# Three-stage layer tower on one core: the attention's output product in column halves with two transposes back to rows, and GpSimd's adds, one expert layer and one transpose moved

## The reference

```python
h = tok(x, mask)                       # running counts per skill, four features, a linear map to 64
h = h + attn(layernorm(h))             # linear attention with decay 0.97
h = h + ffn(layernorm(h))              # 8 experts, the best 2 weighed by a softmax, exact GELU
```

```python
x_t    = l1_normalised(0.97 * x_state + relu(v @ Dx.T))
a_star = rho @ x_t
y_t    = relu(ln(a_star) @ Dy.T) * relu(x_t)
v_star = ln(y_t @ E.T)                 # the product that the change touches
rho    = 0.97 * rho + ln(v)[:, :, None] * x_t[:, None, :]
```

## Time and profile before

| | |
|---|---|
| median of three runs | 813.21 us |
| the profiled execution | 814.54 us |
| its span | 812.7 us |
| TensorE busy | 689.5 us, 85% |
| VectorE busy | 655.8 us, 81% |
| ScalarE busy | 353.4 us, 43% |
| GpSimd busy | 284.0 us, 35% |
| one turn in the middle | 19.21 us |
| granted TensorE clock in that turn | full, the 2.4 GHz level |

### The profile page before, as it was taken

One profiled execution on the slowest core, in us unless ns is written; L12 is line 12 of the kernel. 1 busy time (PEld: TensorE's weight loads), 2 busy tenths in 40 slices (PEclk: granted clock), 3 DMA queues, 4 the chain that ended last, 5 costly groups with the idle time before them and its releaser, 6 DMA issues.

```text
span 812.7 us, 17227 instructions
## 1 busy us (share of the span) xinstructions
PE 689.5 (85%) x4254; PEld 407.6 (50%) x4254; DVE 655.8 (81%) x2531; ACT 353.4 (43%) x787; POOL 284.0 (35%) x333
## 2 busy tenths in 40 slices
PE   2663994067899999999999999999999999999876
PEld 1553663045555555555555555555555555555432
DVE  5998885876888888888888888888888888888752
ACT  4001992012455444445545554444454444445543
POOL 1000000012444444444444444444444444444433
PEclk9999995589999999999999999999999999999988
DMA  7000000101333334433333333333333344342223
GB/s 249 15 0 1 0 0 14 33 27 51 79 81 97 97 93 100 95 110 87 85 85 85 85 85 85 85 85 85 85 93 95 92 100 96 97 104 60 60 61 71
DMA packets 45186, 61.06 MB, mean 75 GB/s; under 512 B 21560, under 2 KB 24108, under 8 KB 44652
## 3 DMA queue, kind: packets, MB, share of 16 engines
q1 hardware_dynamic: 43028, 60.13, 28.8%
q10 hardware_dynamic: 1944, 0.66, 0.4%
q0 software_dynamic: 192, 0.01, 0.0%
HBM read 55.77 MB, written 5.02 MB: 75 GB/s over the span
## 4 chain that ended last, share of the span: by engine, by line
PE 64%; DVE 19%; issue 9%; ACT 2%; DVEq 2%; POOL 2%; DMA 1%; ACTq 0%; SPq 0%; POOLq 0%
PE bank L1257 13%; PE bank L1166 13%; PE bank L1222 6%; PE bank L1178 5%; PE bank L1205 4%; PE bank L1275 4%; PE bank L1250 4%; PE bank L1251 3%; DVE h_all L887 3%; DVE same L663 3%; DVE st_h L893 2%; PE bank L1099 2%; PE bank L1110 2%; PE bank L1155 1%; DVE top L928 1%
## 5 line engine op out<-in xcount | busy, mean ns | idle before, releaser
L512 ACT ACTIVATE skill_rows<-bank,b1T,w_scale 128x512 f32<-128x512 f32 x256 | 194.5, 776 | 52.8 <-PE bank L1251 51.6
L1166 PE MATMUL bank<-feat_parts 128*128 128x256 f32 (+3 forms) x512 | 159.6, 446 | 8.7 <-DVE feat_parts L833 7.6
L407 POOL TENSOR_TENSOR feat_parts<-skill_rows 128x512 f32<-128x512 f32 x64 | 80.9, 1265 | 220.5 <-DVE skill_rows L966 220.5
L485 ACT ACTIVATE feat_parts<-bank 128x384 f32<-128x384 f32 (+2 forms) x96 | 36.7, 383 | 212.0 <-DVE feat_parts L839 209.4
L1257 PE MATMUL bank<-skill_rows,w_sb 128*64 128x512 f32 x256 | 125.4, 611 | 0.2
L1258 PE MATMUL bank<-skill_rows,w_sb 128*64 128x512 f32 x256 | 125.4, 611 | 0.0
L1166 PEld LDWEIGHTS bank<-feat_parts 128*128 128x128 f32 x512 | 90.8, 193 | 50.0 <-issue 20.2
L374 POOL TENSOR_TENSOR same<-h_all,mean_h 128x256 f32 (+1 forms) x32 | 19.5, 608 | 164.7 <-DVEq L1030 164.6
L833 DVE TENSOR_TENSOR_SCAN feat_parts<-same,feat_parts 128x512 f32<-128x512 f32 x64 | 74.6, 1207 | 0.0
L1222 PEld LDWEIGHTS bank<-eT,feat_parts 128*128 128x128 f32 x512 | 64.7, 192 | 4.3
L1222 PE MATMUL bank<-eT,feat_parts 128*128 128x64 f32 x512 | 65.7, 272 | 0.0
(11 more groups left out here) (249 smaller groups left out, 1332.6 us busy)
## 6 DMA issues: line engine op xcount, KB each, us to landing
same<-factor_d SPq DMA_DIRECT2D x32, 512.0 KB, 4.4
skill_rows<-w_d SPq DMA_DIRECT2D x32, 512.0 KB, 6.2
feat_parts<-w_d SPq DMA_DIRECT2D x32, 512.0 KB, 6.1
skill_rows<-skill_row_d SPq DMA_DIRECT2D x4, 1024.0 KB, 7.8
out<-o_sb SPq DMA_DIRECT2D x32, 128.0 KB, 6.3
w_sb<-in_L_ffn_W ACTq DMA_DIRECT2D x2, 256.0 KB
w_d<-wT SPq DMA_DIRECT2D x32, 16.0 KB, 1.4
table_k<-table_d SPq DMA_DIRECT2D x9, 2.5 KB
```

What stands on the lines that cost most here:

```text
L407: pool.tensor_tensor(half[:, n, :], tm[:, 2 * n, :], tm[:, 2 * n + 1, :], ALU.add).then_inc(po_half, 1)
L512: act.activation(hid[:, e, :], h_bank[e % 2][:, :], ACT.Gelu, bias=b1T[:, e:e + 1], scale=w1_scale[:, e:e + 1]).then_inc(ac_gelu, 1)
L1166: last = pe.matmul(n_bank[sc % 2][:, 0:WIDE[sc]], xs[:, k, sc * P:(sc + 1) * P], xs[:, k, sc * P:S], start=(k == 0), stop=(k == NK - 1))
```

## The change

- `z_out` turns the product round: `eT` is stationary and the gated state moves, 256 columns (tokens) at a time; the first 256 tokens go to the lower 64 partitions of bank `az`, the other 256 to the upper 64. A new ScalarE step `z_T` copies this to `zT_sb`, and a new TensorE step `z_rows` transposes it back to rows with two 128x128 transposes, behind expert pairs 2 and 3 and ahead of the logits. `z_copy` waits for these.
- In GpSimd's turn `add_pairs(i - 4, 1)` and `add_halves(i - 4)` stand behind `z_scale` and `centred`, where they stood ahead of each.
- On TensorE `hidden(k, 4)` goes ahead of `values`, `weights_T` ahead of `y_core`, and `centred_T`, which stood between the halves of `z_out`, ahead of it.

```diff
@@ GpSimd, turn
+                if res:
+                    z_scale(i - 1)
+                    centred(i - 1)
                 if done:
                     add_pairs(i - 4, 1)
-                if res:
-                    z_scale(i - 1)
-                if done:
                     add_halves(i - 4)
-                if res:
-                    centred(i - 1)
                 if ahead:
                     centred_input(i + 1)
@@ ScalarE
+            def z_T(b):
+                act.wait_ge(pe_zT, b + 1)
+                wait(act, pe_z, b)
+                act.activation(zT_sb[:], az[:, 0:2 * P], ACT.Copy).then_inc(ac_zT, 1)
...
                 if att:
+                    z_T(i)
                     z_copy(i)
@@ TensorE
-            def z_out(b, chunks):
+            def z_out(b):
                 pe.wait_ge(dv_y, 2 * NK * (b + 1))
-                for c in chunks:
-                    for k in range(NK):
-                        last = pe.matmul(az[:, c * D:(c + 1) * D], ys[:, k, c * P:(c + 1) * P], eT[:, k, :],
-                                         start=(k == 0), stop=(k == NK - 1))
-                if c == C - 1:
-                    last.then_inc(pe_z, 1)
+                for k in range(NK):
+                    for n in range(2):
+                        last = pe.matmul(az[n * D:(n + 1) * D, 0:2 * P], eT[:, k, :],
+                                         ys[:, k, n * 2 * P:(n + 1) * 2 * P], start=(k == 0), stop=(k == NK - 1))
+                last.then_inc(pe_zT, 1)
+
+            def z_rows(b):
+
+                pe.wait_ge(ac_zT, b + 1)
+                for c in range(2):
+                    z = az[:, 0:C * D].rearrange("p (n c d) -> p c n d", n=2, c=2)[:, c]
+                    last = pe.transpose(z, zT_sb[:, c * P:(c + 1) * P], ident_f[:])
+                last.then_inc(pe_z, 1)
@@ TensorE, turn
                     hidden(k, 3, 1 - side)
+                    hidden(k, 4, 1 - side)
                 if att:
                     values(i)
                 if mlp:
-                    hidden(k, 4, 1 - side)
                     expert_out(k, 0)
                     expert_out(k, 1)
-                if att:
-                    y_core(i)
                 if rt:
                     weights_T(t)
+                if att:
+                    y_core(i)
...
-                if att:
-                    z_out(i, range(0, C // 2))
                 if res:
                     centred_T(r)
                 if att:
-                    z_out(i, range(C // 2, C))
+                    z_out(i)
                 if mlp:
                     expert_out(k, 2)
                     expert_out(k, 3)
+                if att:
+                    z_rows(i)
                 if res:
                     logits(r, 1 - side)
```

More of the change, by code:

```diff
@@ L174, in program @@
         power = sb("power", [P, C])
+        zT_sb = sb("zT_sb", [P, 2 * P])
         zv_sb, eps_a = sb("zv_sb", [P, C * D + C]), sb("eps_a", [P, C])
@@ L224, in program @@
         ac_gelu, ac_tanh, ac_wT = sem("ac_gelu"), sem("ac_tanh"), sem("ac_wT")
-        ac_z = sem("ac_z")
+        ac_z, pe_zT, ac_zT = sem("ac_z"), sem("pe_zT"), sem("ac_zT")
         dv_x, dv_diag, dv_y, dv_h = sem("dv_x"), sem("dv_diag"), sem("dv_y"), sem("dv_h")
@@ L543, in turn @@
                     gelu(k, 2)
-                if mlp:
                     gelu(k, 3)
@@ L855, in gate @@
                 dve.wait_ge(pe_y, 2 * b + half + 1)
-                wait(dve, pe_z, b)
+                wait(dve, pe_zT, b)
                 core = n_bank[half][:, :].rearrange("p (k c n) -> p k c n", k=NK, c=2)
@@ L1298, in turn @@
                 if mlp:
-                    hidden(k, 4, 1 - side)
                     expert_out(k, 0)
                     expert_out(k, 1)
+                if rt:
+                    weights_T(t)
                 if att:
                     y_core(i)
-                if rt:
-                    weights_T(t)
                 if mlp:
```

## The result

The changed kernel takes 783.54 us (median of 4 runs, 781.08 to 784.75) against 813.28 of the kernel before on the same chip: 0.963 of it, 95% interval 0.961 to 0.965. The forecast was 789.3, with a range from 784.0: the direction and the mechanism were right, the size was not, 29.7 us instead of 23.9, and the time lies 0.5 us under the range. Spans: 812.7 before, 782.2 after.

What follows compares the result with a forecast made beforehand. TensorE's issued work plus two waits (0.79 and 0.34 us) was taken to bound the 19.21 us turn. Terms summed to -0.89 a turn, -24.9 over 28 turns, +1.0 outside: 789.3 us from the median 813.21, range 784 to 802.

Steps and rivals of the forecast that it cites:

- term 1: Output product on TensorE, in two column halves: 1.06 us instead of 1.82, so -0.76 a turn; bounds 0.94 and 1.82.
- term 2: Two added f32 128x128 transposes on TensorE: +0.32 us a turn, with no wait for zT's copy; bounds 0.2 and 0.66.
- term 5: Weights' transpose ahead of the query product: the 0.34 us wait before the fold goes, -0.34 a turn; bounds 0 and -0.34.
- 3, wait at the value product: GpSimd's adds behind the centring: VectorE's diagonal block comes earlier, TensorE's 0.79 us wait goes, -0.79 a turn.
- 4, wait before layer 4: Layer 4 ahead of the value product: TensorE waits for layer 2's activation, +0.68 us a turn; bounds 0.04 and 0.8.
- the margin that I thought the smallest: At the fold: GpSimd's moved adds give their sum at 12.4 us, TensorE comes at 12.54, in time by 0.15 only.
- Rival A: VectorE's weighing and GpSimd's moved adds exclude each other: fold 1.35 us late, +0.46 a turn, 827 us; 5%.
- Rival B: GpSimd's pair add runs into VectorE's first scan: up to +0.85 us a turn, 813 us; 8%.
- Rival C: Output product's column-half weight loads don't overlap: 2.04 us instead of 1.06, +0.98 a turn, 817 us; 4%.
- Outside the loop's turns: Turns other than the 28 full ones: +0.2 us in turn 3, +0.8 in turn 32, nothing in turns 0 to 2.
- Turn 2 was said to be covered: In turns 0 to 2 TensorE waits for scans, so the extra hop was claimed to be covered, at no cost.
- The tail: Turn 32: moved adds enter the chain to the fold, VectorE's waits of 1.4 us leave; +0.8, bounds -0.4 and +2.6.

## Why the prediction was right or wrong

The step that failed is the sum of a turn, above all term 1, the output product: forecast at 1.06 us, it took 0.91. Of the 0.25 us a turn that the forecast was short, this is 0.15, term 2 is 0.05, and 0.07 was not in the sum; term 5 gave 0.02 too much. What each term measured, from the rows after against the earlier trace rows:

| | predicted | measured |
|---|---|---|
| 1, output product | -0.76 | 1.82 to 0.91: -0.91 |
| 2, two transposes | +0.32 | 0.27 |
| 3, wait at the value product | -0.79 | -0.79 |
| 4, wait before layer 4 | +0.68 | 0.68 |
| 5, wait at the fold | -0.34 | 0.34 to 0.02: -0.32 |
| other rows, not priced | 0 | -0.07 |
| sum | -0.89 | -1.14 |

**Term 1** took 1.06 from the query product, as the row of the same width. That row has a passage on each side, from column halves and to the whole array. The new product goes straight on into the expert pairs, which use column halves too, and takes 0.91; with a passage behind it, it takes 1.01, as the run with the x transposes in between shows. The lower bound, 0.94 by half of two expert pairs, was also above it, since those 1.87 us include their own passage. So both ends were read from rows with a cost that the new place doesn't have.

**The other rows.** I had counted the order as free of cost. By passages, layer 4 and the value product together take 1.68 instead of 1.77 and the two sets of expert pairs 1.81 and 1.82 instead of 1.87 each; the x transposes ahead of the product take 0.32 instead of 0.22, and the weights' transpose with the query product 1.32 instead of 1.23. That is minus 0.20 and plus 0.19: the change moved passages about and saved hardly any. The rest, but for rounding, is the fold, 0.87 instead of 0.92 (before, 394.98 up to this row):

```profile
395.90 0.56 PE L1214 MATMUL bank<-ones_d,a_sq 128*128 128x2 f32 x4
```

It has layer 5 ahead and the variances behind in both kernels, so no passage changed there. It takes 0.91 to 0.94 in the runs in which it waits and 0.83 to 0.87 in those in which it doesn't, so this goes with the wait of term 5; why, is open. That each of the other small differences is a passage is read off from their places; the run with the x transposes shows it for the product and its neighbours alone.

**Term 2** was 0.05 too high: two transposes behind each other take 0.27.

**Terms 3 to 5 held**, and so did the margin that I thought the smallest: the adds end 0.13 before the fold, 0.15 was forecast. Rival A did not come about; VectorE's two weighings ran in 1.41 beside the first of the moved adds, which kept its 1.27. Rival B neither: two scans in 2.33, scores unheld. Rival C neither: it gave 2.04 for the output product, and loads and product together take 0.91. The Trainium skill's rule on weight loads, that they overlap running matmuls only where the row group differs (TensorE: Matmul & The Clock Gate, Part 3: Packing small matmuls), would have given C's time, and the measurement goes against it. The eight loads last 0.136 us each, and four passes of 256 columns in one half need 0.86 by the expert pairs, where a pass of 512 takes 0.43. So each half computes nearly all of the time and its loads are hidden behind matmuls; whether behind its own or the other half's, no run tells.

**Outside the loop's turns** the forecast was +1.0, and the sum is near that by luck: about +0.4 in turns 3 to 31 (what 28 turns of 1.14 leave of the 31.6), +2.1 at turn 2, -1.0 in the tail. Turn 3, forecast at +0.2, takes 17.29 us from its first scores to the next where it took 17.27; turn 5 takes 18.30, 0.23 more than the other turns of the loop, which nothing here explains. Turn 2 was said to be covered, and it is not: I had looked at the copy of zT, which is, and not at the weights' transpose, whose cover is expert layers that turn 2 doesn't have. The tail was put at +0.8 and its fold did wait for the adds by 2.25 us; VectorE's shorter chain gave that back (first layer to fold, 10.61 before and 10.66 after). The 1.0 behind it is not clear of what one execution differs from the next: from the first layer of turn 32 to the end, four runs that have the changed kernel's order there (layer 4 back, the weights' transpose back, the passes swapped, the x transposes behind) take 45.5 to 46.8 us, against 45.6 in the changed kernel and 46.6 before.

**The range** was too narrow by a choice: its low end took the low bounds of two terms, gave 783 and was cut to 784; uncut, it would have held the 783.54. With the unpriced rows open by 0.1 a turn either way it should have reached 780.

## What to carry to other kernels

Price a matmul by a row that has the same neighbours, not only the same width: here the passage between work on the whole array and on column halves is about 0.1 us a time, as much as a tenth of such a product. When a step is moved ahead of the work that covered its wait, look in every part of the program for a turn that has the step and not the cover. And undo the parts of a change that works, one at a time: here one part (layer 4 ahead) was worth nothing, half of another (the pair add) could be put back, and with these two undone and turn 2 mended the kernel is 14 us faster than with the whole change.

## What the runs showed of the hardware that I had not expected

- Work in two column halves overlaps nearly fully, weight loads included, and in both orders that were run: 8 f32 passes of 256 columns take 0.91 us with the halves turn about and 0.92 with one half's four passes ahead of the other's, where four passes alone need 0.86.
- A passage between whole array and column halves costs about 0.1 us in either direction, by the run with the x transposes behind the product.
- The same order of work met a fallen clock in some executions and not in others: in turn 2, behind a wait of 1.26 us, the granted clock is 0.50 in the changed kernel's trace and 1.00 in that with the passes swapped. That costs 1.1 us in turn 2.
- The exclusion of VectorE and GpSimd costs nothing where the held engine has idle time behind it: 0.65 us of it came back with the pair add and the turn got shorter.
